# Softmax sums folded into the value products of three narrow attentions

## The chip, the cores and the metric

The kernel runs on one core of a Trainium2 chip, in one launch. The metric is device time in microseconds. The core has five engines that run their own queues in order: TensorE (PE), VectorE (DVE), ScalarE (ACT), GpSimd (POOL) and SyncE (SP, which issues DMAs). They meet through semaphores.

## What is computed

A stack of four layers over x of shape [4, 512, 128]; each is a cross attention to a short context of 154 rows a batch, followed by a mixture of experts. Three of the four cross attentions (layers 0, 2 and 3) are narrow: 16 heads of 8 columns. With layer norm and per-layer details (rotary tables and norms of q and k in layer 0, a mask in layer 2) cut, each of them is

```
q, k, v = split_heads(xn @ Wq), split_heads(ctx @ Wk), split_heads(ctx @ Wv)   # 16 heads of 8
attn    = softmax(einsum('bhqd,bhkd->bhqk', q, k) * scale, axis=-1)            # 512 x 154 a head
out     = einsum('bhqk,bhkd->bhqd', attn, v)                                   # 512 x 8 a head
x       = x + tanh(gate) * (out.reshape(B, T, 128) @ Wo + bo)
```

The softmax needs a row maximum ahead of the exponential and a row sum behind it. The other layer (1) has a wide attention, and layer 2 a causal one besides; the change doesn't touch them.

## The kernel before

`narrow_attention` is called three times, with names that begin with L0x ("rope"), L2x ("mask") and L3x ("plain"). It works through four batches b = 0 to 3. The 16 heads are four groups c of four heads; head j of a group sits in rows 32j to 32j+31. For one batch there are these pieces, and the order of PE's queue is written out by hand:

- **Scores for the maxima** (`scores`, L1149): twelve units a batch, eight of three row tiles and four of two, for the *next* batch f = b + 1. Every unit goes to the same two PSUM banks (0 and 1), so unit n waits for the DVE maximum (`maxima`, L1611) of unit n-1. I call the twelve units of a batch S0 to S11; S2, S5, S8 and S11 are the short ones.
- **Maxima turned** (`max_rows`, L1158 on PE, L1396 on ACT, then a DMA into row 9 of the query tile), so that the transposed scores come out with the maximum subtracted.
- **Transposed scores** (`scoresT`, L1175, and L1177 for the tail of 26 context rows) in five slots c = 0 to 4 of four heads each, slot 4 being the tails of all 16 heads; banks 2 to 5. ACT takes the exponential of each (`exps`, L1404) into `pT`.
- **Value products** (`products`, L1198): four matmuls a slot, 128 rows by 32 columns each, into bank OUT = 6. The weights `vz` hold 8 value columns at head c's place in a 32-column window and zeros elsewhere, so the four slots pile up in one bank.
- **Sums** (`sums`, L1210): the same four matmuls once more, with weights of ones (`oz`, and `ot` for the tail), into bank SUMS = 7. Each sum comes out 8 times, in the rows of its own head.
- **Normalising**: ACT copies both banks out (`values`, L1412 and L1413, to `ov` and `rsum`), DVE inverts and multiplies per tile t of 128 rows (`normalised`, L1622 and L1626), PE multiplies by Wo (`output`, L1225), DVE adds the residual (`added`, L1634) and takes the statistics (`kept_in_parts`).

In batch b the PE queue is: T0, P4 of the batch before, S0, max_rows, sums 4, rowsT, S1, T1, P0, S2, queries, sums 0, S3, T2, S4, P1, S5, sums 1, T3, S6, P2, output, S7, max_rows, sums 2, S8, T4, S9, P3, S10, sums 3, S11 (T and P being `scoresT` and `products` of a slot). The last batch has no S pieces. In layers 0 and 3 it also carries the first steps of the experts' router, whose DVE work stands behind `normalised` in DVE's queue and which `output` waits for. DVE's queue in a batch is the twelve maxima with the normalising of the batch before put between them. Each layer begins and ends at a barrier of all engines.

At the start of a layer ACT fills the query tiles with ones and `vz` with zeros (L1418), POOL makes regrouped weights (L990 or L992) and clears the key tile (L994), and DVE writes values into `vz` (L1561) and `vt` (L1562).

## Time and profile before

| | us |
|---|---|
| three runs | 1573.18, 1577.87, 1580.15 |
| median | 1577.87 |
| span of the profiled execution (its device time is not given apart from that) | 1592.2 |
| span above the median | 14.3 |
| L0x, first scores to the last residual added | 39.5 to 189.5 |
| L2x, the same | 738.7 to 874.4 |
| L3x, the same | 1317.5 to 1458.4 |
| mean granted TensorE clock | 0.900 |

### The profile page before, as it was taken

What the parts mean: (1) busy time and instruction counts of PE and PEld (TensorE: products, weight loads), DVE (VectorE), ACT (ScalarE), POOL (GpSimd) and SP (SyncE); (2) the same over time, 40 slices, a digit from 0 to 9 for tenths busy, and PEclk for the clock granted to TensorE, in tenths of its full rate; (3) what the DMA queues carried; (4) which work ended last, traced back from release to release, by engine and by line L of the source; (5) the groups of instructions that cost most, each with busy time, mean ns of one, the idle gap of its engine ahead of it and who ended that gap; (6) DMA issues with size and microseconds to landing.
All of it is one profiled execution on the core that took longest, in us unless ns stands there. A gap on an engine that the chain in (4) does not pass through costs nothing. (4 is left out here: it accounts for less than half of the span.)

```text
span 1592.2 us, 25277 instructions
## 1 busy us (share of the span) xinstructions
PE 1297.0 (81%) x8946; PEld 752.5 (47%) x8946; DVE 946.5 (59%) x2139; ACT 723.1 (45%) x1940; POOL 527.5 (33%) x625
## 2 busy tenths in 40 slices
PE   2799629579989977784997698989887977996998
PEld 2444317345656645463442455656554434442443
DVE  6466621444555655255664688888764875555664
ACT  3354413166656533342543465655755333454222
POOL 2320340525333361333100365656643320000444
PEclk8599859799999997895998799999988996998999
DMA  2444120330000002322000000000000001000000
GB/s 65 127 130 128 40 66 26 72 75 14 1 1 2 1 27 62 89 58 50 9 10 2 1 1 1 1 2 1 1 1 1 1 10 23 10 3 1 7 7 14
DMA packets 66991, 45.30 MB, mean 28 GB/s; under 512 B 17564, under 2 KB 60261, under 8 KB 66869
## 3 DMA queue, kind: packets, MB, share of 16 engines
q1 hardware_dynamic: 61013, 34.48, 8.4%
q0 software_dynamic: 4096, 8.40, 1.9%
q8 instruction: 74, 1.21, 0.3%
q10 hardware_dynamic: 1760, 0.82, 0.3%
q14 instruction: 48, 0.39, 0.1%
HBM read 24.91 MB, written 13.89 MB: 24 GB/s over the span
## 5 line engine op out<-in xcount | busy, mean ns | idle before, releaser
L3411 ACT ACTIVATE L2a_pr<-psum,L2a_negmax 128x512 f32<-128x512 f32 (+3 forms) x256 | 132.6, 532 | 94.0 <-DVE L2a_negmax L3537 40.1
L557 ACT ACTIVATE L1x_praw<-psum,L1x_negmax 128x154 f32<-128x154 f32 x256 | 96.5, 392 | 78.4 <-DVE L1x_negmax L649 78.2
L318 POOL TENSOR_TENSOR L1x_pm<-L1x_praw,L1x_total 128x1024 f32<-128x1024 f32 x32 | 60.7, 1898 | 160.6 <-DVE L1x_total L655 111.7
L3276 PE MATMUL psum<-ident,L2a_pr 128*128 128x128 f32 x640 | 85.9, 278 | 19.0 <-DVE L2a_pT L3550 11.7
L649 DVE TENSOR_REDUCE L1x_negmax<-psum 128x4 f32<-128x616 f32 x64 | 50.7, 794 | 55.2 <-PE psum L370 51.0
L3276 PEld LDWEIGHTS psum<-ident,L2a_pr 128*128 128x128 f32 x640 | 71.7, 143 | 24.7 <-issue 21.1
L1978 POOL TENSOR_TENSOR L3f_scaled<-L3f_sg,L3f_wide 128x512 f32<-128x512 f32 (+1 forms) x44 | 55.7, 1271 | 66.9 <-ACT L3f_sg L2057 37.9
L1611 DVE TENSOR_REDUCE L3x_negmax<-psum 128x6 f32<-128x924 f32 (+1 forms) x48 | 47.7, 1011 | 46.8 <-PE psum L1149 37.4
L1611 DVE TENSOR_REDUCE L0x_negmax<-psum 128x6 f32<-128x924 f32 (+1 forms) x48 | 47.8, 1010 | 44.9 <-PE psum L1149 40.6
L3161 POOL TENSOR_TENSOR L2a_pr<-L2a_pr,L2a_total 128x1024 f32<-128x1024 f32 x29 | 56.5, 1947 | 46.5 <-DVE L2a_total L3566 46.3
L3164 POOL TENSOR_TENSOR L2a_pr<-L2a_pr,L2a_total 128x768 f32<-128x768 f32 x32 | 48.7, 1520 | 70.0 <-DVE L2a_total L3566 69.7
L1611 DVE TENSOR_REDUCE L2x_negmax<-psum 128x6 f32<-128x924 f32 (+1 forms) x48 | 47.8, 1011 | 32.6 <-PE psum L1149 27.8
L1404 ACT ACTIVATE L3x_pT<-psum 128x512 f32<-128x512 f32 x80 | 41.4, 606 | 50.3 <-PE psum L1175 41.8
L1404 ACT ACTIVATE L2x_pT<-psum 128x512 f32<-128x512 f32 x80 | 41.4, 605 | 49.0 <-PE psum L1175 40.5
L2057 ACT ACTIVATE L3f_sg<-psum 128x512 f32<-128x512 f32 (+1 forms) x44 | 26.3, 598 | 66.8 <-PE psum L2000 66.8
L3556 DVE COPY L2a_pT<-psum 128x768 f32<-128x768 f32 (+1 forms) x64 | 54.2, 846 | 3.3 <-PE psum L3276 3.3
L370 PE MATMUL psum<-L1x_kT,L1x_qT 64*128 64x154 f32 x512 | 52.6, 327 | 3.9 <-ACT L1x_qT L538 3.0
L1404 ACT ACTIVATE L0x_pT<-psum 128x512 f32<-128x512 f32 x80 | 41.4, 605 | 30.2 <-PE psum L1175 23.6
L3411 ACT ACTIVATION_READ_ACCUMULATOR L2a_pr<-psum,L2a_negmax 128x1 f32 x256 | 53.5, 209 | 0.0
L557 ACT ACTIVATION_READ_ACCUMULATOR L1x_praw<-psum,L1x_negmax 128x1 f32 x256 | 52.9, 207 | 0.0
L2878 PE MATMUL psum<-L1f_gu,L1f_xsT 128*128 x92 | 51.2, 645 | 1.1 <-ACT L1f_xsT L2931 1.1
L2000 PE MATMUL psum<-L3f_xnT,expert_arena 128*128 128x512 f32 (+1 forms) x88 | 46.7, 614 | 4.2 <-PEq L3822 4.2
(741 smaller groups left out, 3372.1 us busy)
## 6 DMA issues: line engine op xcount, KB each, us to landing
expert_arena<-in_L_ffn_w SPq DMA_DIRECT2D x16, 256.0 KB, 4.4
group_in<-zero SPq DMA_DIRECT2D x2, 1472.0 KB, 9.3
L1f_xs<-group_in SPq DMA_DIRECT2D x10, 256.0 KB, 3.8
group_out<-L1f_ys SPq DMA_DIRECT2D x10, 256.0 KB, 3.6
L1f_gu<-in_L_ffn_gate_up_w SPq DMA_DIRECT2D x8, 256.0 KB, 3.5
slots_in<-zero SPq DMA_DIRECT2D x1, 1280.0 KB, 9.0
L0f_xs<-slots_in SPq DMA_DIRECT2D x5, 256.0 KB, 3.6
resid<-in_x SPq DMA_DIRECT2D x4, 256.0 KB, 5.8
```

The source lines that it names most:

```text
L318: nc.gpsimd.tensor_tensor(pm[:, n % 2].rearrange("p j t k -> p (j t) k"), praw[:, n % 3, :, :, 0:MAIN].rearrange("p j t k -> p (j t) k"), ...
L370: last = nc.tensor.matmul(psum[:, 2 * u + j, x * CTX:(x + 1) * CTX], qT[rows, g, t * P:(t + 1) * P], kT[rows, g, :], start=True, stop=True)
L557: nc.scalar.activation(praw[:, n % 3, j, t, :], psum[:, 2 * u + j, x * CTX:(x + 1) * CTX], ACT.Exp, bias=negmax[:, n % 2, u, j, x:x + 1], ...
L649: nc.vector.tensor_reduce(negmax[:, n % 2, u].rearrange("p j x -> p (j x)").rearrange("p (j x) -> p j x", x=2), psum[:, 2 * u:2 * u + 2, 0 ...
L1404: nc.scalar.activation(pT[:, (n % 2) * NG + j, :], psum[:, LANES + j, :], ACT.Exp, scale=scale).then_inc(s["pt"], 1)
L1611: nc.vector.tensor_reduce(negmax[:, f % 2, half, 2 * h:2 * h + 2, off:off + count], psum[:, bank:bank + 2, 0:count * CTX].rearrange("p j ( ...
L1978: nc.gpsimd.tensor_tensor(scaled[0:rows, n % 2, :], sg[0:rows, n % 3, :], wide[0:rows, picked_to(n) % SLANT, :], ALU.mult).then_inc(s["sca ...
L2878: nc.tensor.matmul(psum[:, UP[i % len(UP)], :], xsT[:, q % 2, t * P:(t + 1) * P], w["gu"][:, bass.ds(expert[i], 1), :].rearrange("p a f -> ...
L3161: ins = nc.gpsimd.tensor_tensor(x, x, inv[:, 0:2].unsqueeze(2).to_broadcast([P, 2, SEQ]), ALU.mult)
L3276: last = nc.tensor.transpose(psum[:, TURN + n // 4, n % 4 * P:(n % 4 + 1) * P], pr[:, m % RING, n * P:(n + 1) * P], core.ident[:])
L3411: ins = nc.scalar.activation(pr[:, i % RING, SEQ * j + lo:SEQ * j + hi], psum[:, bank + j, lo:hi], ACT.Exp, bias=negmax[:, i % RING, e:e + ...
L3556: nc.vector.tensor_copy(pT[:, q % 2, t:t + 7:3, heads, :], src[:, :, 0:3 * P].rearrange("p j (k x) -> p k j x", x=P))
```

## The change

The sums get no matmuls of their own. A 32-column window of `vz` has 24 columns that hold zeros; head group c now has ones in the eight columns of its neighbour c ^ 1, so that one matmul gives values and sum. Two groups would then write into each other's rows, so groups 0 and 2 go to bank EVEN = 6 and groups 1 and 3 to bank ODD = 7. In each bank half of the rows hold values and the other half sums, for the head group next door. The tail is split in the same way: `vt` is used in two halves of 64 rows, one for each bank, 8 matmuls in place of 4.

Behind it: ACT reads EVEN twice with a row mask as its scale (`half`), once for the sums and once for the values; DVE adds the ODD bank to each with the opposite mask (`odd_merged`, two scalar_tensor_tensor of 128x512); one stream shuffle of 128x512 brings each sum to its head's rows; the reciprocals stay four of 128 columns inside a batch and are two of 256 in `all_normalised`; the multiplications become two of 256 columns. In DVE's queue these are spread over the maxima anew. In PE's queue `output` moves from before S7 to behind it. POOL fills `vt` with its pattern of ones first thing in each layer, and ACT fills `vz` in four pieces from a bfloat16 pattern `windows`.

```diff
-    LANES, OUT, SUMS = 2, 6, 7
+    TAIL_AT = (0, 2, 1, 3)
+    LANES, EVEN, ODD = 2, 6, 7
...
             def _(pool):
+                nc.gpsimd.tensor_copy(vt[:].rearrange("p f j x a d -> p (f j) x (a d)"),
+                                      core.pairs[:].unsqueeze(1).unsqueeze(3).to_broadcast([P, B * NG, 2, 2 * DK])).then_inc(s["vt_ones"], 1)
                 pool.wait_ge(loaded, 16 * n_loads)
...
                         if b:
-                            pe.wait_ge(s["ov"], 2 * b - 1)
+                            pe.wait_ge(s["even"], 2 * b)
...
+                    if c == 1:
+                        if b:
+                            pe.wait_ge(s["odd"], 2 * b)
+                        elif rope:
+                            pe.wait_ge(s["kc"], 2)
                     for j in range(NG):
-                        x = c * P + 32 * j
-                        nc.tensor.matmul(psum[32 * j:32 * j + 32, OUT, :], vz[:, b, x:x + 32] if c < NG else vt[:, b, j].rearrange("p c d -> p (c d)"),
-                                         pT[:, (n % 2) * NG + j, :], start=(c == 0), stop=(c == NG))
-
-                def sums(b, c):
...
-                    for j in range(NG):
-                        last = nc.tensor.matmul(psum[32 * j:32 * j + 32, SUMS, :], core.oz[:, c, :] if c < NG else core.ot[:].rearrange("p c d -> p (c d)"),
-                                                pT[:, (n % 2) * NG + j, :], start=(c == 0), stop=(c == NG))
+                        own = slice(32 * j, 32 * j + 32)
+                        p = pT[:, (n % 2) * NG + j, :]
+                        if c < NG:
+                            x = (NG * b + c) * P + 32 * j
+                            last = nc.tensor.matmul(psum[own, EVEN + c % 2, :], vz[:, x:x + 32], p, start=(c < 2), stop=False, skip_group_check=True)
+                        else:
+                            for a in range(2):
+                                rows = slice(64 * a, 64 * a + 64)
+                                last = nc.tensor.matmul(psum[own, EVEN + a, :], vt[rows, b, j].rearrange("p x a d -> p (x a d)"), p[rows, :],
+                                                        start=False, stop=True, skip_group_check=True)
                     last.then_inc(s["pv"], 1)
...
                     for t in range(QT):
-                        pe.wait_ge(s["on"], QT * b + t + 1)
+                        if t % 2 == 0:
+                            pe.wait_ge(s["on"], 2 * b + t // 2 + 1)
...
                     products(b, 2)
+                    scores(f, 7, 8)
                     if b and not ends:
                         output(b - 1, lane(b, 3, 1))
-                    scores(f, 7, 8)
                     if f < B:
                         max_rows(2 * f, lane(b, 3, 0))
-                    sums(b, 2)
...
-                    nc.scalar.activation(ov[:], psum[:, OUT, :], ACT.Copy).then_inc(s["ov"], 1)
-                    nc.scalar.activation(rsum[:], psum[:, SUMS, :], ACT.Copy).then_inc(s["ov"], 1)
+                    nc.scalar.activation(rsum[:], psum[:, EVEN, :], ACT.Copy, scale=core.half[:, 1:2]).then_inc(s["even"], 1)
+                    nc.scalar.activation(ov[:], psum[:, EVEN, :], ACT.Copy, scale=core.half[:, 0:1]).then_inc(s["even"], 1)
...
-                def normalised(b, t0, t1):
+                def odd_merged(b, k):
...
+                    nc.vector.scalar_tensor_tensor(out=to[:], in0=psum[:, ODD, :], scalar=core.half[:, k:k + 1], in1=to[:],
+                                                   op0=ALU.mult, op1=ALU.add).then_inc(s["odd"], 1)
...
+                    v.step(nc.vector.stream_shuffle(oT[:], rsum[:], [i ^ DK for i in range(32)]))
...
-                    normalised(b - 1, 0, 1)
+                    odd_merged(b - 1, 0)
                     maxima(f, 2, 3)
-                    normalised(b - 1, 1, 2)
+                    sums_swapped(b - 1)
                     query_squares(g)
                     maxima(f, 3, 4)
+                    odd_merged(b - 1, 1)
+                    inverted_sums(b - 1, 0, 1)
                     maxima(f, 4, 5)
                     query_inverted(g)
-                    normalised(b - 1, 2, 3)
+                    inverted_sums(b - 1, 1, 2)
                     maxima(f, 5, 6)
-                    normalised(b - 1, 3, 4)
+                    normalised(b - 1, 0)
+                    inverted_sums(b - 1, 2, 3)
                     maxima(f, 6, 7)
+                    inverted_sums(b - 1, 3, 4)
+                    maxima(f, 7, 8)
+                    normalised(b - 1, 1)
                     added(b - 1)
```

## Rows read from the trace of the kernel before

**Rows 1.** The page's first part: busy time, share of the span, instructions of each engine.

```profile
PE 1297.0 (81%) x8946; PEld 752.5 (47%) x8946; DVE 946.5 (59%) x2139; ACT 723.1 (45%) x1940; POOL 527.5 (33%) x625
```

**Rows 2.** Batches 1, 2 of L3x: length; PE, PEld, DVE, ACT, POOL busy; clock; DMA.

```profile
1369.65:1400.14 30.49, 29.38 (x299) 14.11 (x295) 18.99 (x31) 13.79 (x27) 0.00 (x0) 1.00 0.07 12
1400.14:1426.27 26.13, 25.09 (x269) 12.34 (x265) 18.36 (x31) 12.83 (x24) 0.00 (x0) 1.00 0.01 3
```

**Rows 3.** PE in order of time, L3x: start, length, line, operation, idle before.

```profile
1347.27 1.61 PE L1210 MATMUL psum<-L3x_pT,oz 128*32 128x512 f32 x8
...
1369.65 1.05 PE L1149 MATMUL psum<-L3x_k,L3x_q 32*128 32x154 f32 x12
1370.63 0.60 PE L1158 MATMUL psum<-ident,L3x_negmax 128*8 128x128 f32 x4
1371.17 1.06 PE L1210 MATMUL psum<-L3x_pT,ot 128*32 128x512 f32 x8
...
1372.75 1.05 PE L1149 MATMUL psum<-L3x_k,L3x_q 32*128 32x154 f32 x12
...
1380.71 1.05 PE L1149 MATMUL psum<-L3x_k,L3x_q 32*128 32x154 f32 x12 [0.36 <-DVE L3x_negmax L1611]
...
1382.99 0.79 PE L1149 MATMUL psum<-L3x_k,L3x_q 32*128 32x154 f32 x8 [0.23 <-DVE L3x_negmax L1611]
...
1387.54 1.16 PE L1225 MATMUL psum<-L3x_wo,L3x_oT 128*128 128x128 f32 x8
1388.63 1.05 PE L1149 MATMUL psum<-L3x_k,L3x_q 32*128 32x154 f32 x12
...
1391.14 0.79 PE L1149 MATMUL psum<-L3x_k,L3x_q 32*128 32x154 f32 x8
1391.87 1.14 PE L1177 MATMUL psum<-L3x_q,L3x_k 32*32 32x512 f32 x32
1392.94 1.05 PE L1149 MATMUL psum<-L3x_k,L3x_q 32*128 32x154 f32 x12
```

**Rows 4.** DVE in order of time, L3x batch 1, same columns.

```profile
1381.81 1.12 DVE L1611 TENSOR_REDUCE L3x_negmax<-psum 128x6 f32<-128x924 f32 x1 [1.16 <-PE psum L1149]
1382.85 0.94 DVE L1622 RECIPROCAL L3x_rsum<-L3x_rsum 128x128 f32<-128x128 f32 x1
1383.83 0.29 DVE L1626 TENSOR_TENSOR L3x_oT<-L3x_ov,L3x_rsum 128x128 f32<-128x128 f32 x1
...
1388.74 0.75 DVE L1634 SCALAR_TENSOR_TENSOR L3x_oT<-psum,gate,resid 128x512 f32<-128x512 f32 x1 [0.89 <-PE psum L1225]
```

**Rows 5.** Groups of one line, L2133 (experts of layer 3): count, busy us, mean ns.

```profile
L2133 DVE STREAM_SHUFFLE L3f_wide<-L3f_shares 128x512 f32<-128x512 f32 x36 | 26.1, 727 | 0.0
```

**Rows 6.** DVE in order of time, L0x batch 0: first squares of the queries.

```profile
74.29 0.69 DVE L1569 TENSOR_TENSOR L0x_ra<-L0x_qf 128x512 f32<-128x512 f32 x1 [0.90 <-ACT L0x_qf L1361]
```

**Rows 7.** L3x batch 3 in order of time: DVE, then PE.

```profile
1433.34 3.35 DVE L1622 RECIPROCAL L3x_rsum<-L3x_rsum 128x512 f32<-128x512 f32 x1 [4.20 <-ACT L3x_rsum L1413]
...
1437.87 1.13 PE L1225 MATMUL psum<-L3x_wo,L3x_oT 128*128 128x128 f32 x8 [2.25 <-DVE L3f_lg L1875]
1449.51 1.04 PE L1210 MATMUL psum<-L3x_pT,ot 128*32 128x512 f32 x8
1455.56 2.05 PE L1225 MATMUL psum<-L3x_wo,L3x_oT 128*128 128x128 f32 x8 [5.01 <-DVE L3x_oT L1626]
```

**Rows 8.** Busy time by stretch, last batch of L2x.

```profile
850.10:853.50 3.40, 1.34 (x12) 1.25 (x16) 2.66 (x6) 0.26 (x1) 0.00 (x0) 1.00 0.00 0
853.50:856.90 3.40, 3.40 (x20) 0.60 (x20) 2.33 (x11) 1.75 (x4) 0.00 (x0) 0.50 0.02 5
```

**Rows 9.** Start of L2x in order of time: POOL, PE; below, POOL at 758.

```profile
711.82 0.39 POOL L992 COPY L2x_wqp<-L2x_wq 128x128 f32<-128x128 f32 x1 [16.58 <-POOLq L3820]
712.36 1.11 PE L1052 MATMUL psum<-L2x_wk,ctxp 128*80 128x128 f32 x4 [4.70 <-POOL L2x_wqp L992]
758.84 1.27 POOL L1040 TENSOR_TENSOR resid<-resid,L2x_gbo 128x512 f32<-128x512 f32 x1 [0.68 <-DVE L2x_xn L1537]
```

More of the change, by code:

```diff
@@ L177, in _ @@
                 last.then_inc(parts_made, 1)
+                dve.wait_ge(consts, 7)
+                nc.vector.tensor_reduce(core.half[:], core.hmask[:].rearrange("p (x a) -> p a x", a=2), X_AXIS, ALU.add)
                 dve.wait_ge(ctx_made, 2)
@@ L1176, in scoresT @@
                             else:
-                                last = nc.tensor.matmul(psum[32 * x:32 * x + 32, LANES + j, :], k4[rows, x, b, MAIN:KP], q4[rows, b % QB, x, :],
+                                to = 32 * TAIL_AT[x]
+                                last = nc.tensor.matmul(psum[to:to + 32, LANES + j, :], k4[rows, x, b, MAIN:KP], q4[rows, b % QB, x, :],
                                                         start=True, stop=True)
@@ L1269, in _ @@
                     pe.wait_ge(s["bvb"], 1)
-                    nc.tensor.matmul(psum[:, OUT, 0:D], bvb[:], w["wo"][:], start=True, stop=True).then_inc(s["bias_ps"], 1)
+                    nc.tensor.matmul(psum[:, EVEN, 0:D], bvb[:], w["wo"][:], start=True, stop=True).then_inc(s["bias_ps"], 1)
                 for b in range(B):
@@ L1308, in _ @@
                     scores(f, 5, 6)
-                    sums(b, 1)
                     scoresT(b, 3)
@@ L1328, in _ @@
                     scores(f, 10, 11)
-                    sums(b, 3)
                     scores(f, 11, 12)
@@ L1334, in _ @@
                 products(B - 1, NG)
-                sums(B - 1, NG)
                 if dispatch:
@@ L1417, in _ @@
                 filled(0)
-                nc.scalar.activation(vz[:].rearrange("p f e -> p (f e)"), core.oneb[:, 0:1].to_broadcast([P, B * NG * WIDE]), ACT.Copy,
-                                     scale=0.0).then_inc(s["vz_zero"], 1)
+                for f in range(B):
+                    nc.scalar.activation(vz[:, f * NG * P:(f + 1) * NG * P].rearrange("p (c j e) -> p c j e", c=NG, j=NG),
+                                         core.windows[:].unsqueeze(2).to_broadcast([P, NG, NG, 32]), ACT.Copy).then_inc(s["vz_ones"], 1)
                 if rope:
@@ L1735, in _ @@
                         router.spread(dve, v)
-                    maxima(f, 9, 10)
                     normed(b + 3)
@@ L1745, in _ @@
                     router.front_first(dve, v, xns[0])
-                normalised(b - 1, 0, QT)
+                all_normalised(b - 1)
                 if router:
@@ L1758, in _ @@
                     router.best(dve, v, 0, 1, 1)
-                normalised(B - 1, 0, QT)
+                all_normalised(B - 1)
                 if dispatch:
```

92 lines of the change are left out of this document (53 added, 39 removed).

## The prediction

> **What bounds the kernel now.** I read the page first: PE is busy for 81% of the span, more than any other engine [rows 1]. That is an average, and the change sits in three stages only, so the next view is the busy time by stretch of two batches of layer 3's attention [rows 2]. There PE is busy 29.38 of 30.49 us and 25.09 of 26.13 us, DVE 19 and 18. By that share every matmul taken out would come off the time. The third view, PE in order of time, says otherwise [rows 3]. Between one score unit and the next stands a piece of filler, and where the filler is a single piece PE idles 0.36 or 0.23 us until DVE's maximum frees the banks. S4 starts at 1380.71 and S5 at 1382.99: 2.28 us a long unit, and that is 0.99 of PE, 1.12 of DVE's maximum [rows 4] and some 0.17 of handing over. This ping-pong over two banks is a second bound right under PE. Eight long units at 2.28 and four short ones at about 1.75 (0.72 + 0.80 and the handing over; S8 to S9 takes 1.80 [rows 3]) make 25.2 us a batch, against the 30.49 and 26.13 measured. So of a batch's sums only what stands in a gap that is longer than its 2.28 or 1.75 can come off.
>
> **What goes.** A group of sums takes 1.0 us of PE at the high clock (1371.17 to the next piece at 1372.16, by its 1.06 less the overlap) and about 1.55 at the low one [rows 3]. There are 5 x 4 x 3 = 60: 59 us of PE's time.
>
> *Gap by gap, L3x batch 1* (S0 at 1369.65, the next at 1400.14, 30.49 [rows 2, 3]). S0 to S1 is 3.10 with max_rows, sums and rowsT; without sums it is 2.11 of PE's work, so the ping-pong's 2.28: -0.8. S1 (1372.75) to S4 (1380.71) is 7.96 [rows 3]: T1 and P0 fill the first gap to 2.9, `queries` and sums the second to 2.8, the third is the ping-pong's 2.28. The second falls to 1.8, its own 0.72 and 1.06 of `queries`: -1.0. S5 (1382.99) to S7 (1388.63) is 5.64 [rows 3], 2.7 with sums and T3 and 2.95 with P2 and `output`; the first falls to 1.75: -0.9. Sums 3 stand alone behind S10 in a gap of 2.28: 0. Sums 2 stand behind S7 and are dealt with below.
>
> **What DVE gets.** A batch had four reciprocals of 0.94 and four multiplications of 0.29: 4.9 us [rows 4]. Now there are two merges from PSUM, by the one like instruction 0.75 each [rows 4]; a shuffle, 0.73 by 36 of the same shape [rows 5]; the reciprocals; and two multiplications of 256 columns, between 0.29 and 0.69 (a 512-column one [rows 6]), say 0.42. Sum 6.8: +1.9 us. Beside a unit's 0.99 of PE and 0.17 there is room for 1.15 of DVE work in each long gap and 0.9 in each short one. Put where the diff puts them: the first merge and the shuffle fit. Behind maximum 3 stand a merge and a reciprocal, 1.7: the maximum of S4 starts 0.6 late, so the gap S4 to S5 grows from 2.28 to 2.9: +0.6. Behind maximum 5, 0.42 + 0.94 makes 0.3 more in the gap S6 to S7. The other reciprocals fit within 0.1.
>
> **The output's new place.** `output` leaves the gap S6 to S7, which falls from 2.95 to 2.28 + 0.3: -0.35. It now stands behind S7, and its second half needs the second multiplication, which DVE's queue has behind maximum 7. After S7's start that maximum ends at 2.3 and the multiplication at 2.75; only then come half of `output` (0.55), max_rows (0.53) and S8: 3.9 us for a gap that was 1388.63 to 1391.14, 2.51 [rows 3]. +1.4. PE waits there for DVE for 1.3 us in a place where it waited for nothing; behind the wait are max_rows, whose DMA has some 8 us in hand, and S8.
>
> Batch 1 in sum: -0.8 - 1.0 - 0.9 + 0.6 + 0.1 - 0.35 + 1.4 = about -1.0. The waits on `even` cost nothing: both ACT reads end about 1 us before P0 comes up, as they stood on ACT ahead of slot 1's exponentials already; `odd` is up 0.2 us before P1. In layer 0 the removal behind `queries` gives nothing, as maximum 3 waits there for the squares of the queries, which wait for ACT's copy [rows 6]; I take -0.5. Batch 2 has no `queries` and no rowsT: -0.2 - 0.8 - 0.35 + 0.6 + 1.4 = +0.6. Batch 0 has nothing to normalise: -2.7 in L3x (its first sums run at the low clock, 1.6 [rows 3]), -1.8 in L2x, where DVE has late rows to finish in the same place, -1.2 in L0x. Over three layers: batch 0 -5.7, batch 1 -2.5, batch 2 +1.8: **-6.4**.
>
> **The last batch.** No maxima here; the chain is DVE, then `output`, then T2 and the exponentials. `output` of batch 2 waited for a 512-column reciprocal (3.35), four multiplications (0.9) and the router's first step [rows 7]. `all_normalised` is merge 0.75, shuffle 0.73, merge 0.75, then twice a 256-column reciprocal (half of 3.35, 1.7) and 0.42: 6.5 in place of 4.25, and it starts about 0.7 earlier (ACT's sums are read first, and sums 4 are gone): T2 comes +1.5 late. From T2 on, PE's three pieces a slot become two, and the pace goes over to ACT's 2.07 for four exponentials: from T2 to the end of the last products 9.7 us in place of 11.6 to the end of the last sums (1438.9, the end of `output`, to 1450.5 [rows 7]). The tail behind that, from 1450.5 to `output`'s end at 1457.6 [rows 7], grows by 2.25 of DVE, less 0.5 for the order of ACT's reads: 1.6 with the two tiles of `output` that are still to come. 1.5 - 1.9 + 1.6: Sum +1.2 a layer: **+3.5**.
>
> **The clock.** In the last batch of L2x PE is busy for 1.34 us of 3.4 while it waits for `output`, and the next 3.4 us are granted 0.50; L3x idles there 2.25 us and keeps 1.00 [rows 7, 8]. With PE's wait now about 5 us long, cut by half an `output`, I expect the low clock in L3x and L0x too and a longer one in L2x. In the low stretch PE is busy throughout [rows 8], so 3.4 us at half speed lose up to 1.7: bounds 0 and 1.7 a layer, twice that for a second stretch. I take 1.5 each: **+4.4**.
>
> **The layer's start.** POOL's new copy of 512 columns stands first in its queue. In L2x PE's first matmul waits 4.70 us for POOL's L992 right behind it [rows 9]; in L3x and L0x ACT, DVE and SP wait for the pieces that follow on POOL in much the same way. A copy of 128 columns takes 0.39, a two-input one of 512 takes 1.27 [rows 9]: between 0.4 and 1.3, I take 1.15, since this is a strided one of 512. **+3.4**. ACT's four short fills in place of a long one I cost at nothing: the same columns, and the first is ready sooner.
>
> **The tail products.** Eight matmuls of 64 rows by 32 columns in place of four of 128 by 32. The nearest row is the tail of the transposed scores, sixteen of 32 by 32 with the same moving columns: 1391.87 to 1392.94, 1.07 us, as much as four full ones [rows 3]. So 0, with +1.0 each (12 in all) as the upper bound if the two row halves don't run side by side. The Trainium skill, TensorEngine Tiling (Array Packing), Key Properties, says that a change of tiling mode drains TensorE. The row doesn't show it: S8, T4 and S9 follow each other by 0.73 and 1.07 us across two such changes. By the page every removed group of sums would save two drains and the new 64-row mode would add none over the mode it replaces, so that it would speak for the change, by an amount that no row prices.
>
> **Sum.** -6.4 + 3.5 + 4.4 + 3.4 = +4.9 us, taken on the profiled execution, whose span of 1592.2 stands 14.3 above the median of the runs; all terms are stretches between barriers, so I put them on the median: 1577.9 + 4.9 = about 1583.
>
> **Rivals.** *PE is the bound after all* (faster). It would need the 1.9 us of DVE work to slip in without delaying a maximum and the wait before `output`'s second half to be short. For it: PE's 96% [rows 2]. Then batch 0 gives -5.7, batch 1 about -3 and batch 2 about -1.7 a layer, the last batch -2: 5.7 + 9 + 5 + 6 = 26 us, 1552; half of that, if one of the two holds, 1565. Against it: PE's idle times that end on DVE [rows 3]. It decides if S7 to S8 stays under 2.5 us. Chance 0.16. *The low clock spreads* (slower). Inside batches 1 and 2 PE's share falls from 96% to some 83%, with a wait of 1.3 us behind S7; if the grant falls there too, each of six batches pays a stretch like that in [rows 8], 1.7 us and the slower pieces after it, 2.5: +15, 1598. For it: the grant did fall on a share of 0.39. Against it: 83% is far above that. It decides from one lost stretch in every second batch. Chance 0.14. *The 64-row tail products run one after the other* (slower): +1.0 in 12 gaps, as behind S11 there is more filler than ping-pong: 1595. Chance 0.06. *The forecast*: the sums' 59 us were nearly all cover, and what comes off is given back on DVE. Chance 0.64.
>
> **How the numbers follow.** Within 0.5% (7.9 us, about what a measurement of this kernel can tell from none) is 1570 to 1586. Of the forecast's 0.64, whose own range is 1574 to 1592 by the bounds of copy, clock and multiplications, I put 0.46 inside, 0.17 above, 0.01 below. The first rival is faster, the other two slower. Faster 0.17, same 0.47, slower 0.36. The range 1567 to 1598 leaves out most of the first rival and the far end of the second.
>
> **What the profile after would show.** No L1210 group; S0 to S1 at 2.28; S2 to S3 at 1.8 in L2x and L3x; S4 to S5 at 2.9; S7 to S8 at 3.9 with PE waiting for the multiplication; DVE busy some 2 us more a batch; `output` of batch 2 in the last batch 1.5 us later, and the granted clock at 0.50 behind it in all three layers; PE's first matmul in L2x and L3x 1.15 us later; tail products 1.0 us. The prediction is wrong if PE hardly idles in batches 1 and 2, if the low clock lasts longer, or if waits for which the trace names no releaser move with the changed queues, which I can't price.

## The result and the profile after

The kernel after takes 1587.74 us, the median of 10 runs (1579.39 to 1598.27), beside 1577.25 for the kernel before (10 runs, 1571.47 to 1580.15): ratio 1.0076, interval 1.0053 to 1.01. It is slower by 0.8%. That lies in the range 1567 to 1598 and on the forecast's side of the old time, but about twice as far from it as the 4.9 us of the sum: outside the 0.5% that were given the largest of the three chances (0.47), and in the class that was given 0.36. Medians here and below are over all runs; ratios and intervals compare each kernel with the kernel before run beside it (medians 1575.57 to 1577.25), and leave out the few runs that are over 1.5% above the fastest of their kernel.

The first part of the page for the profiled execution after, which answers to [rows 1]:

```profile
span 1583.9 us, 24590 instructions
...
PE 1270.8 (80%) x8562; PEld 756.4 (48%) x8562; DVE 969.6 (61%) x2183; ACT 723.8 (46%) x1949; POOL 532.8 (34%) x627
```

PE has 384 matmul records fewer and is only 26 us less busy; DVE is 23 us busier. The mean granted clock fell from 0.900 to 0.882. The two spans as wholes can't be set against each other, because the span before is 14 us above its own median. The excess lies outside the change: from the last residual of L0x to the first maximum of L2x that execution takes 551.2 us, and the twelve other traces of this study take 527.1 to 532.3. So I compare stretches.

Busy time by stretch. First the kernel after, two rows for each of L0x, L2x and L3x: batch 1, from its first maximum to the next batch's, and the last batch, from the last maximum to the end of the statistics of the last rows. Columns: stretch and length; PE, PEld, DVE, ACT, POOL busy with counts; clock; DMA share and GB/s.

```profile
98.75:133.05 34.30, 29.59 (x276) 16.69 (x275) 23.07 (x38) 17.20 (x31) 5.05 (x5) 0.85 0.41 114
158.68:199.53 40.85, 27.41 (x226) 13.49 (x220) 28.37 (x87) 18.69 (x32) 9.92 (x10) 0.76 0.09 25
772.43:802.77 30.34, 26.56 (x264) 14.07 (x263) 20.41 (x33) 13.80 (x26) 0.00 (x0) 0.94 0.07 13
828.47:864.31 35.84, 21.09 (x146) 6.79 (x142) 18.38 (x39) 13.32 (x25) 0.00 (x0) 0.74 0.00 1
...
1359.53:1389.87 30.34, 26.56 (x264) 14.07 (x263) 20.40 (x34) 13.81 (x26) 0.00 (x0) 0.94 0.07 12
1415.50:1452.09 36.59, 21.83 (x158) 8.55 (x153) 22.39 (x58) 14.83 (x27) 0.00 (x0) 0.73 0.01 1
```

The same stretches of the kernel before, without L3x's batch 1, which is the first row of [rows 2] (counted there from score unit to score unit, with the same length):

```profile
97.83:130.62 32.79, 30.62 (x308) 15.42 (x307) 22.43 (x35) 17.31 (x31) 5.06 (x5) 1.00 0.46 118
156.42:191.48 35.06, 26.52 (x258) 12.01 (x252) 24.32 (x81) 18.56 (x32) 9.28 (x10) 0.90 0.09 27
787.46:817.95 30.49, 29.38 (x296) 14.11 (x295) 18.99 (x32) 13.79 (x26) 0.00 (x0) 1.00 0.07 12
843.81:876.22 32.41, 22.18 (x178) 6.91 (x172) 14.31 (x33) 12.94 (x25) 0.00 (x0) 0.86 0.00 1
1427.11:1460.26 33.15, 22.19 (x190) 8.28 (x184) 18.33 (x52) 14.62 (x27) 0.00 (x0) 0.91 0.00 1
```

Two things are to be seen. In batch 1 of L3x, PE lost 2.8 us of work (29.38 to 26.56) and the batch lost 0.15 us: the rest is idle time, and the clock of the stretch went from 1.00 to 0.94. And the three last batches together grew from 100.62 to 113.28 us, 12.7 us, with a clock of 0.73 to 0.76 in place of 0.86 to 0.91. More than the whole loss sits there. A second trace of the same queue order (the section on the start of the layer) has each of the three within 0.5 us of these.

PE in order of time in the second half of L3x's batch 1, after (answers to [rows 3]; the times in brackets are idle time ahead, and who ended it):

```profile
1374.12 1.05 PE L1154 MATMUL psum<-L3x_k,L3x_q 32*128 32x154 f32 x12 [0.30 <-DVE L3x_negmax L1618]
...
1376.73 0.71 PE L1232 MATMUL psum<-L3x_wo,L3x_oT 128*128 128x128 f32 x4 [0.91 <-DVE L3x_oT L1652]
...
1377.81 0.79 PE L1154 MATMUL psum<-L3x_k,L3x_q 32*128 32x154 f32 x8
...
1382.13 1.05 PE L1154 MATMUL psum<-L3x_k,L3x_q 32*128 32x154 f32 x12 [0.23 <-DVE L3x_negmax L1618]
1384.47 0.45 PE L1154 MATMUL psum<-L3x_k,L3x_q 32*128 32x154 f32 x2 [1.29 <-DVE L3x_negmax L1618]
...
1385.48 1.92 PE L1180 MATMUL psum<-L3x_q,L3x_k 32*128 32x512 f32 x6
1387.33 1.43 PE L1216 MATMUL psum<-L3x_pT,L3x_vt 64*32 64x512 f32 x16
1388.70 1.05 PE L1154 MATMUL psum<-L3x_k,L3x_q 32*128 32x154 f32 x12
```

S7 to S8 is 3.69 us, 0.91 of it the wait for the second multiplication, as forecast (3.9 and 1.3). The new thing is at the end: behind S10, where sums 3 stood, PE idles 1.29 us, and the transposed scores after it take 1.92 us for six records that took 1.02 at the high clock. S11 (1384.47) to the next S0 (1388.70) is 4.23 us, 2.6 before. The windows of that place and of three places in the last batch:

```profile
1384.70:1388.10 3.40, 3.40 (x24) 1.35 (x30) 0.80 (x1) 1.46 (x4) 0.00 (x0) 0.50 0.00 0
1415.40:1418.80 3.40, 3.40 (x26) 0.33 (x18) 2.00 (x6) 2.49 (x4) 0.00 (x0) 0.50 0.00 0
1425.70:1432.50 6.80, 4.67 (x20) 2.50 (x24) 5.76 (x20) 0.52 (x2) 0.00 (x0) 0.50 0.01 2
1442.70:1452.10 9.40, 2.42 (x8) 1.86 (x8) 7.90 (x17) 0.00 (x0) 0.00 (x0) 0.50 0.00 1
```

The last batch of L3x in order of time, PE, after (answers to [rows 7]):

```profile
1422.33 1.06 PE L1212 MATMUL psum<-L3x_pT,L3x_vz 128*32 128x512 f32 x8
1427.83 2.05 PE L1232 MATMUL psum<-L3x_wo,L3x_oT 128*128 128x128 f32 x8 [4.44 <-DVE L3f_lg L1914]
1429.81 2.09 PE L1180 MATMUL psum<-L3x_q,L3x_k 32*128 32x512 f32 x8
...
1446.18 1.20 PE L1232 MATMUL psum<-L3x_wo,L3x_oT 128*128 128x128 f32 x4 [5.23 <-DVE L3x_oT L1652]
```

PE stands 4.44 us ahead of `output` where it stood 2.25 us, then runs `output` and the scores of slot 2 at half speed. The releaser is the router's copy on DVE, but that copy waits only for its place in DVE's queue behind `all_normalised`, whose instructions run back to back from 1421.20:

```profile
1421.20 0.75 DVE L1628 SCALAR_TENSOR_TENSOR L3x_rsum<-psum,half,L3x_rsum 128x512 f32<-128x512 f32 x1 [3.66 <-ACT L3x_rsum L1413]
...
1427.17 0.43 DVE L1652 TENSOR_TENSOR L3x_oT<-L3x_ov,L3x_rsum 128x256 f32<-128x256 f32 x1
1427.51 0.22 DVE L1914 COPY L3f_lg<-psum 128x68 f32<-128x68 f32 x1
```

### The profile page after: what moved, and what is told of

Read it like the earlier page. It is cut to its first block and busy times, and to the rows that moved or that the text cites. A ratio compares the mean times of both kernels' runs of the same rounds, so it can differ in the third digit from the quotient of the medians.

```text
span 1583.9 us, 24590 instructions
## 1 busy us (share of the span) xinstructions
PE 1270.8 (80%) x8562; PEld 756.4 (48%) x8562; DVE 969.6 (61%) x2183; ACT 723.8 (46%) x1949; POOL 532.8 (34%) x627
## 5 line engine op out<-in xcount | busy, mean ns | idle before, releaser
L1154 PE MATMUL psum<-L0x_k,L0x_q 32*128 32x154 f32 x384 | 39.3, 337 | 17.3 <-DVE L0x_negmax L1618 11.6
L1154 PEld LDWEIGHTS psum<-L0x_k,L0x_q 32*128 32x128 f32 x384 | 30.2, 207 | 43.9 <-DVE L0x_negmax L1618 31.6
```

What stands on the lines that cost most here:

```text
L1154: last = nc.tensor.matmul(psum[:, bank + j % 2, k * CTX:(k + 1) * CTX], q4[rows, f % QB, c, t * P:(t + 1) * P], k4[rows, c, f, 0:CTX], sta ...
```

## The experiments

I began with two theories. **A**: the low clock gives the gain back; PE, relieved of the sums, idles in places where it was busy, and what follows runs at 0.50. **B**: the DVE work that was added, and `output`, which now waits for it, cost the time. Each run lists its span and mean granted clock, so I also use the time that a run spent at the low clock: 2 x span x (1 - clock), as 1.00 and 0.50 are the two levels. For the profiled execution after that is 2 x 1583.9 x 0.118 = 374 us.

### The sums' places filled again

The kernel after, with four matmuls of zero weights (adding zero to a value bank) at each of the places where sums 0 to 3 stood:

```diff
+    def cover(b, c):
+        for j in range(NG):
+            nc.tensor.matmul(psum[32 * j:32 * j + 32, EVEN + c % 2, :], core.zero[:, 0:32],
+                             core.ctxp[:].rearrange("p b k -> p (b k)")[:, 0:SEQ], start=False, stop=False, skip_group_check=True)
```

> The changed kernel with four groups of matmuls with weights of zeros, added into the same banks, at the places where sums 0 to 3 stood (48 groups of 60; the result is the same). The profiles show the granted clock low for 208 us inside the three narrow attentions after the change and for 140 before. Theory A, the clock: the loss comes from stretches at 1.2 GHz that follow PE's new idle time. Then the covers bring the low time back to some 140 to 160 us and the time down from 1587.7 to 1577 to 1583, although PE has 48 us more to do. Theory B, DVE and the waits: the loss is DVE's added work and output's wait. Then the covers give nothing or cost up to 10 us: 1587 to 1598.

1593.71 us (6 runs, 1588.15 to 1596.82), ratio 1.0103, interval 1.0084 to 1.0122. The low clock did leave: 325 us of it in the median run in place of 374, none in batch 1 of L3x. But that batch is longer:

```profile
1366.92:1398.27 31.35, 28.49 (x296) 14.03 (x295) 20.41 (x34) 13.80 (x26) 0.00 (x0) 1.00 0.07 12
```

31.35 us at the full clock, against 30.34 after and 30.49 before. With about the PE work of before and the DVE work of after the batch loses 0.9 us to the kernel before, with no low clock in it: that is theory B's part. One gap outweighs what the others gain: S7 to S8 takes 4.68 us (2.51 before), as `output`, its wait and the filler now all stand there. So A alone is out, and a filler that costs PE as much as the sums did is no cure.

### The sums dropped, nothing added

The kernel before with sums of slot 0 only, by weights of ones (the products of the later slots signal ACT in their place); the sums of slots 1 to 4 are left out, and the probabilities are divided by wrong sums. (The weights have to be ones in all columns: with `oz` as it was, three quarters of the sums would be zero and not all inverses finite.)

```diff
-                    if n < 0:
+                    if n < 0 or c:
                         return
...
-                nc.gpsimd.memset(core.oz[:], 0.0).then_inc(groups, 1)
+                nc.gpsimd.memset(core.oz[:], 1.0).then_inc(groups, 1)
```

> The kernel before, with its softmax sums made for slot 0 alone, by weights that are all ones (slots 1 to 4 are left out, so the probabilities are divided by wrong sums); nothing is added on VectorE, ScalarE or GpSimd, and the output is issued where it was. It is the change's gain without its cost on the other engines. From the gaps between maxima of batch 1 in the kernel before and after, sums cost 0.3 to 1.0 us at each of their places, 3.4 us a batch, and there is no second wait of the output: with the clock as before, some 9 us a layer, 1549 us. Theory A (the clock takes back what the freed TensorE gives): low clock appears in batches 0 and 1 and in the last batches here too, as VectorE's work is not needed for it; low-clock time in the three attentions goes from 140 us to over 190, and the time is 1556 to 1566. Theory B (the time after is set by VectorE's added work and the later output): low-clock time stays under 160 us and the time is 1545 to 1553.

1570.49 us (8 runs, 1559.76 to 1582.12), ratio 0.9976, interval 0.9947 to 1.0004. That is outside what either theory expected: 48 of the 60 groups of sums, 48 us of PE's work by the prediction's 1.0, taken out for nothing and with the queues in their old order, are worth 5 us in the median, and not even that is certain. The windows of the profiled execution, L3x: batch 1, then the last batch in two parts.

```profile
1342.25:1370.99 28.74, 25.37 (x264) 13.31 (x263) 19.00 (x32) 13.62 (x26) 0.00 (x0) 1.00 0.07 13
1395.70:1415.78 20.08, 15.43 (x134) 5.79 (x128) 11.58 (x36) 13.37 (x25) 0.00 (x0) 1.00 0.01 2
1415.78:1426.61 10.83, 3.11 (x16) 1.94 (x16) 6.76 (x16) 1.09 (x3) 0.00 (x0) 0.69 0.00 0
```

Batch 1 falls by 1.75 us only, for 4.0 us of PE's work: two bounds close to each other, as the prediction had it (PE 25.37 of 28.74 busy, the rest idle behind maxima). This execution, at 1560.32, is among its kernel's fastest: 15 us under the kernel before, with about its low-clock time (320 us by the trace). Over the eight runs low-clock time has a median of 336 us against 312 for the kernel before (61 runs), so part of A shows here without any DVE work, and by the two numbers the low clock takes back a good part of what the removal gives.

### The DVE work alone

The kernel before, with two merges and a shuffle a batch added to DVE in L2x and L3x (reading and writing spare tiles), PE untouched:

```diff
+                    src = core.ctxp[:].rearrange("p b k -> p (b k)")[:, 0:SEQ]
+                    v.step(nc.vector.scalar_tensor_tensor(out=core.x1[:, 8:12, :].rearrange("p n d -> p (n d)"), in0=src, scalar=core.gate[:, 0:1], in1=src, op0=ALU.mult, op1=ALU.add))
...
+                    v.step(nc.vector.stream_shuffle(core.x1[:, 8:12, :].rearrange("p n d -> p (n d)"), core.ctxp[:].rearrange("p b k -> p (b k)")[:, 0:SEQ], [i ^ DK for i in range(32)]))
```

> The kernel before with DVE's added work alone in layers 2 and 3: two scalar_tensor_tensor and a shuffle of 128x512 into a tile that nobody reads, near the places where the change has them; PE's queue untouched. 2.2 us more of DVE in each of eight batches. Theory A: PE stays busy, so batches 1 and 2 grow by 0.6 each and the last by 2 x 2.2 a layer: 2 x (1.2 + 4.4) = 11 us at most, half of it if PE's own pace hides it: 1583 to 1588, with the low clock within 10 us of before. Theory B: the same 11 us or more, and it is the whole of the loss: 1588 to 1592. It tells how large DVE's share is.

1581.16 us (7 runs), ratio 1.0034, interval 1.0017 to 1.005: some 5.5 us for two layers. Low-clock time stays at 310 us in the median run. In L3x batch 1 goes from 30.49 to 30.55 and batch 2, which has less PE filler, from 25.80 to 26.98 (from its first to its last maximum):

```profile
1380.60:1407.58 26.98, 24.82 (x266) 12.17 (x266) 20.33 (x36) 12.01 (x22) 0.00 (x0) 1.00 0.01 2
```

So B's cost is real, of that order, and has nothing to do with the clock.

### The start of the layer

The kernel after, with POOL's pattern copy moved from the head of its queue to behind the clearing of `k4`:

```diff
-                nc.gpsimd.tensor_copy(vt[:].rearrange("p f j x a d -> p (f j) x (a d)"),
-                                      core.pairs[:].unsqueeze(1).unsqueeze(3).to_broadcast([P, B * NG, 2, 2 * DK])).then_inc(s["vt_ones"], 1)
                 pool.wait_ge(loaded, 16 * n_loads)
...
                 nc.gpsimd.memset(k4[:], 0.0).then_inc(s["k_zero"], 1)
+                nc.gpsimd.tensor_copy(vt[:].rearrange("p f j x a d -> p (f j) x (a d)"),
+                                      core.pairs[:].unsqueeze(1).unsqueeze(3).to_broadcast([P, B * NG, 2, 2 * DK])).then_inc(s["vt_ones"], 1)
```

> The kernel after, with GpSimd's copy that fills the tail tiles with their pattern moved behind the clearing of k4, so that it no longer stands ahead of the layer's first work on that queue. The prediction gave it 3.4 us for three layers. If that is right: 1584 against the 1587.5 of the kernel after. If it is hidden, as the two prologues in the traces say (L3x 33.35 before and 32.60 after): 1586 to 1589, and each prologue within 0.5 us of the kernel after where the clock is the same.

1586.7 us (4 runs, 1582.21 to 1590.92), ratio 1.0075, interval 1.0052 to 1.0098: not to be told from the kernel after. In the trace after, PE's first matmul of L2x waits 5.30 us behind POOL, where it waited 4.70 [rows 9]:

```profile
702.75 1.11 PE L1057 MATMUL psum<-L2x_wk,ctxp 128*80 128x128 f32 x4 [5.30 <-POOL L2x_wqp L997]
```

With the copy moved it is 4.72 again. So the copy costs this wait 0.6 us, its own length (0.61 us on GpSimd), half of the 1.15 forecast. With four runs a term of 1 to 2 us in all can't be excluded; 3.4 looks too much.

### The idle places filled

The kernel after, with five of the zero-weight groups (5 x 4 matmuls) ahead of the `output` that PE waits for in the last batch:

```diff
                     if ends:
+                        for _ in range(5):
+                            cover(b, 0)
                         output(b - 1, 1)
```

> The changed kernel with five groups of zero-weight matmuls in the last batch of each narrow attention, between P0 and output, where PE otherwise waits for DVE. Theory A: of the low time in the last batches (19.7, 18.8 and 19.5 us in the three layers after, 7 to 9 before) some 7 to 10 us a layer go, and the time falls by 5 to 10 us: 1578 to 1583. Theory B: the fills stand in a wait for DVE and change nothing: 1586 to 1590.

1590.78 us (5 runs, 1583.95 to 1592.37), ratio 1.0085, interval 1.0062 to 1.0107: no gain. Yet the last batches in its profile did what they should:

```profile
161.44:198.82 37.38, 26.38 (x266) 12.02 (x260) 28.15 (x87) 18.69 (x32) 9.46 (x10) 0.87 0.09 26
838.01:871.44 33.43, 22.57 (x186) 7.84 (x180) 18.38 (x39) 13.32 (x25) 0.00 (x0) 0.81 0.01 1
1423.41:1457.49 34.08, 22.39 (x198) 8.90 (x192) 22.39 (x58) 14.77 (x27) 0.00 (x0) 0.87 0.00 1
```

104.89 us in place of 113.28. The 8.4 us came back elsewhere: low-clock time was 372 us in the median run, as before the edit (374). The profiled execution is the median one, and beside the trace of the kernel after it shows where: 2 to 4 us more in each batch 1 of L0x and L2x and in batch 2 of L3x, all with more low clock (12.0 us of it in L2x's batch 1 where there were 3.4), and 4 us more between L0x and L2x. Then both: the last batch filled, and one group between S10 and S11 of every batch.

```diff
                     scores(f, 10, 11)
+                    cover(b, 3)
                     scores(f, 11, 12)
```

> The kernel after, with matmuls of zero weights (four of 512 columns for one group, adding zero) at two places: one group between scores 10 and 11 of every batch, where TensorE idles 1.29 us and behind which the low clock began in batch 1, and five groups ahead of the last batch's output. Theory A (the low clock gives back what the change gains): the gap S11 to S0 in batch 1 goes from 4.13 (4.51 in L0x) to 2.93, no low clock in batch 1, the three last batches as in the kernel with the last groups alone (35.6, 32.7, 32.3 us from the last maxima on), so some 8 us there and 4 us in the batches: 1575 to 1580. Theory B (VectorE's work and the output's wait): the filling work only costs, 1588 to 1594. Rival to both: the low clock moves to a place that is not filled (batch 0, the prologue), its sum in the attentions stays near 208 us and the time is 1584 to 1590.

1589.65 us (6 runs, 1575.24 to 1597.03), ratio 1.0104, interval 1.0074 to 1.0133. The profiled execution is the fastest of the six and shows the place as A had it: the filler costs nothing (S10 to S11 is 2.35 us, 2.34 without it), and the transposed scores behind it run at full speed.

```profile
1376.10 1.05 PE L1154 MATMUL psum<-L3x_k,L3x_q 32*128 32x154 f32 x12 [0.23 <-DVE L3x_negmax L1626]
1377.09 1.06 PE L1222 MATMUL psum<-ctxp,zero 128*32 128x512 f32 x8
1378.45 0.40 PE L1154 MATMUL psum<-L3x_k,L3x_q 32*128 32x154 f32 x2 [0.30 <-DVE L3x_negmax L1626]
...
1380.03 1.09 PE L1216 MATMUL psum<-L3x_pT,L3x_vt 64*32 64x512 f32 x16
1381.05 1.05 PE L1154 MATMUL psum<-L3x_k,L3x_q 32*128 32x154 f32 x12
```

```profile
1353.51:1382.22 28.71, 25.93 (x272) 13.64 (x271) 20.39 (x34) 13.80 (x26) 0.00 (x0) 1.00 0.07 13
```

The batch is 28.71 us in place of 30.34 with one low stretch less: 1.6 us is what one stretch cost. But the median of the kernel did not move; its other runs had mean clocks down to 0.878. The rival that was written down, that the low clock turns up where nothing is filled, is what the medians say. Where it went in those slower runs of this kernel no trace shows, since only the profiled one has a trace.

### The second multiplication earlier

```diff
+                    normalised(b - 1, 1)
                     maxima(f, 7, 8)
-                    normalised(b - 1, 1)
                     added(b - 1)
```

> The kernel after, with the second multiplication of the normalised rows (L1652) issued on VectorE before maxima 7 in place of behind them, so that the output in batches 1 and 2 need not wait its 0.91 us for it (gap S7 to S8 3.42 us). Theory B (this wait and the order on VectorE set the time): the gap falls to about 2.6, 0.8 us in each of 6 batches is gained, 1583. Theory A (the clock takes it back): the gap falls, but low-clock time moves to another place, 1585 to 1589. A third outcome: maxima 7 come later by the 0.42 us of the multiplication, scores behind them wait, and the gap before is longer by what this one is shorter.

1573.19 us (10 runs, 1565.1 to 1592.07), ratio 0.9992, interval 0.9963 to 1.0021. I ran it again:

> The kernel with the second multiplication ahead of maxima 7 once more, beside the two that move the output, since its runs spread from 1565 to 1592. If its median of 1573.2 holds, 1570 to 1577 here, and the spread goes with the mean granted clock of each run: some 0.4 us of span for each us of low clock.

1573.76 us (12 runs, 1565.71 to 1590.51), ratio 0.9975, interval 0.9954 to 0.9996. One swap of two instructions on DVE gives back all that the change lost, 14 us, more than either theory expected. The first of its two traces says how. `output` is one piece again, right behind S7, and batch 1 runs at the full clock:

```profile
1363.79 1.05 PE L1154 MATMUL psum<-L3x_k,L3x_q 32*128 32x154 f32 x12 [0.30 <-DVE L3x_negmax L1618]
1364.78 1.16 PE L1232 MATMUL psum<-L3x_wo,L3x_oT 128*128 128x128 f32 x8
...
1366.30 0.79 PE L1154 MATMUL psum<-L3x_k,L3x_q 32*128 32x154 f32 x8
```

```profile
98.64:130.17 31.53, 27.73 (x276) 16.48 (x275) 22.98 (x38) 17.20 (x31) 5.04 (x5) 0.89 0.42 117
768.84:796.38 27.54, 24.68 (x264) 13.42 (x263) 20.31 (x33) 13.80 (x26) 0.00 (x0) 1.00 0.08 13
1349.19:1376.73 27.54, 24.67 (x264) 13.41 (x263) 20.32 (x33) 13.80 (x26) 0.00 (x0) 1.00 0.08 13
```

S7 to S8 falls from 3.69 to 2.51, so 1.2 us, and the batch from 30.34 to 27.54, 2.8: the other 1.6 is the low stretch at its end, which is gone though nothing was put behind S10. A wait in one place cost clock in another, 8 us later. All traces together bear that out. Take the place behind S10 in batches 1 and 2 of L2x and L3x, four a trace. In the four traces that have both the wait ahead of S8 and the one behind S10 (after, pattern copy moved, last batch filled, output later alone) 13 of 16 such places get a low stretch. In the three that have only the one behind S10 (this edit twice, both edits) none of 12 does, in the two where S10 is followed by filler none of 8, and in the three with the sums' matmuls in place (before, DVE work added, before with the output later) none of 12. With the sums dropped, where PE idles behind S10 too, two of four do. So the wait of 1.3 us is followed by the low clock mostly where 0.9 us were idle ahead of it; what spared the three others isn't shown.

The two traces of this one kernel, 1571.06 and 1584.03, also say where the slower one loses its time. L0x, from its first maximum to its last residual, takes 146.0 us in the first and 165.2 us in the second, with 50 and 90 us of low clock. That is more than the whole difference.

### The output of batch 2 later

In the last batch, `output` was moved from ahead of the scores of slot 2 to behind those of slot 3, in the kernel after, in the kernel after with the multiplication's edit, and in the kernel before:

```diff
-                    if ends:
-                        output(b - 1, 1)
                     scores(f, 3, 4)
...
                     scoresT(b, 3)
+                    if ends:
+                        output(b - 1, 1)
```

> The kernel after, with the output of batch 2, which is issued inside the last batch, moved on TensorE's queue from ahead of scores of slot 2 to behind those of slot 3. In the kernel after TensorE stands 4.44 us (L3x, 1423.39 to 1427.83) ahead of this output, and the scores of slot 2, which need nothing of it, stand behind it. Theory A with its refinement (in the last batches TensorE's queue is held by the output, which is late by VectorE's longer chain; the idle time also brings the low clock): the slots 2 and 3 come 3 to 4 us earlier, exps of the last batch end 2 to 3 us earlier in each of three layers, low-clock time in the last batches falls from 58 us to under 45, and the time is 1575 to 1580. Rival (the order behind it is held by ScalarE's exps anyway, and the later output delays VectorE's work behind it): 1585 to 1590.

1577.09 us (12 runs, 1565.53 to 1592.3), ratio 0.9987, interval 0.9965 to 1.0008. That is some 10 us under the kernel after, as expected. The last batches:

```profile
161.07:201.24 40.17, 25.10 (x226) 11.27 (x220) 28.02 (x87) 18.79 (x32) 10.07 (x10) 0.76 0.09 24
834.25:863.40 29.15, 18.32 (x146) 6.32 (x142) 18.37 (x39) 13.31 (x25) 0.00 (x0) 0.79 0.00 1
1414.49:1444.56 30.07, 19.66 (x158) 7.64 (x153) 22.40 (x58) 14.82 (x27) 0.00 (x0) 0.78 0.01 2
```

6.7 and 6.5 us less in L2x and L3x, 0.7 in L0x. There the move makes a new wait. DVE adds the residual only behind `output`, and the router's mask stands behind that in DVE's queue, so PE now waits for the mask, in this trace for 5.38 us:

```profile
182.90 0.17 PE L2376 MATMUL psum<-L0f_mask,L0f_tri 128*128 128x8 bf16 x1 [5.38 <-DVE L0f_mask L2360]
```

> Both edits: the kernel after with the second multiplication ahead of maxima 7, and the output of batch 2 behind the scores of slot 3 in the last batch. If the two are independent and the idle time of TensorE is what both take away: 1573.2 (the multiplication's edit alone) less some 8 us: 1563 to 1568, under the kernel before. If the clock takes back what is gained: 1570 to 1576.

1564.16 us (6 runs, 1557.49 to 1572.54), ratio 0.9918, interval 0.9889 to 0.9948: the version that beats both. The gains of the two edits nearly add up: 14 and 11 us alone, 23.6 together, from 1587.74. PE in the last batch of L3x has no wait ahead of `output` any more:

```profile
1418.01 2.04 PE L1180 MATMUL psum<-L3x_q,L3x_k 32*128 32x512 f32 x8
1420.10 1.13 PE L1232 MATMUL psum<-L3x_wo,L3x_oT 128*128 128x128 f32 x8
```

> The kernel before with the same move of the output in the last batch, and nothing else. Its idle time ahead of that output is 2.25 us in L3x. If the stall is a cost of its own that the change only made longer: some 1.5 us a layer, 1570 to 1573, so about half of what the same move gives to the kernel after. If it is within the noise: 1574 to 1577.

1573.85 us (12 runs), ratio 0.9992, interval 0.9977 to 1.0006: not to be told from none, at most 3.6 us. The trace shows that this is a sum of two things and not nothing: the last batches of L2x and L3x are 3.8 and 2.3 us shorter than in the kernel before, and that of L0x is 5.8 us longer, with 4.51 us of waiting for the router's mask and 5.5 us more low clock. The kernel after gained 10 us by the same move, since its DVE chain ahead of `output` is longer. The move in L2x and L3x alone, which these numbers suggest for both kernels, was not run.

### The clock over all runs

Medians over the runs of each kernel; low is time at the low clock worked out per run, slope is the span's by it within the runs of that kernel:

```
kernel                        runs   time us   clock            low us   slope
before                          61   1576      0.898 to 0.909   312      0.25
before, output later            12   1573.85   0.896 to 0.907   311      0.22
before, DVE work added           7   1581.16   0.899 to 0.905   310      0.31
before, sums dropped             8   1570.49   0.888 to 0.897   336      0.57
after                           10   1587.74   0.877 to 0.889   374      0.37
after, pattern copy moved        4   1586.70   0.880 to 0.886   368      0.37
after, sums' places filled       6   1593.71   0.895 to 0.903   325      0.32
after, last batch filled         5   1590.78   0.879 to 0.888   372      0.26
after, S10 and last filled       6   1589.65   0.878 to 0.895   368      0.37
after, output later             12   1577.09   0.872 to 0.894   365      0.34
after, multiplication early     10   1573.19   0.879 to 0.897   358      0.40
the same again                  12   1573.76   0.879 to 0.894   351      0.43
after, both edits                6   1564.16   0.880 to 0.893   348      0.35
```

The kernel after has 62 us more low clock than the kernel before. By its own slope that is 23 us, against the 10 to 12 measured: at equal clock the change would have gained some 11 us. This is an estimate, and a loose one: no run of the kernel after had as little as 312 us, and by the slope of the kernel before the 62 us are 16, which leaves a gain of 4. That the slopes are what the low clock costs, and not only what goes with it, is argued and not shown.

## Why the prediction was right, and where its sizes were off

**The sign and the range: right.** The sums' matmuls were mostly cover and not the bound. The dropped sums show it: 48 us of PE's work are 5 us of time in the median and 15 in the profiled execution. That the number came within 6 us owes something to luck, as the batches alone were off by 8 us. The rival *PE is the bound after all* (1552 to 1565) fell.

**The gaps: right to 0.4 us.** S0 to S1 was forecast at 2.28 and is 2.35 (1358.35 to 1360.70); S2 to S3 1.8 and 1.78; S4 to S5 2.9 and 2.49; S7 to S8 3.9 and 3.69, with PE waiting 0.91 for the multiplication where 1.3 was forecast. DVE's batch grew by 1.42 us (18.99 to 20.41), not 1.9. At the full clock batch 1 of L3x takes 28.71 us with the filled idle time: -1.8, where the prediction had -1.0. The trace with the pattern copy moved has it at 28.72 with nothing filled. Batch 2, forecast at +0.6, came out at -0.2.

**The batches' sum: wrong in size.** Forecast -6.4 over three layers. Measured between the two profiled executions, batch 0, 1, 2: L0x -0.8, +1.5, -0.2; L2x +1.3, -0.1, -0.2; L3x +0.3, -0.1, -0.2. Together +1.6. The terms that failed are batches 0 and 1, and not by their gaps but by their clock, which the prediction took to stay as it was: by the clock of the two traces L3x had 18.5 us at the low level in batch 0 where it had had 11.6, and each batch 1 has at least one stretch (0.94 in the windows above, 0.85 in L0x). Batch 0 is the less certain of the two, as it differs between traces of one order: L2x's has no low clock in the trace before and 7.1 us of it, and 2.8 us more time, in that of the kernel before with the output later. The lost stretches of batch 1 are the rival *the low clock spreads*. So are those behind S10 of batch 2 in L2x and L3x, which the windows above count with the last batch (1415.40:1418.80 in L3x). Five of its six batches have one; the price is 1.6 us for the one that could be measured alone, not 2.5. Its 14% were too few: the argument against it weighed the share of a whole batch (83%), and the grant fell behind S10, where PE now waits 1.29 us in a gap that the prediction had put at nothing, some 8 us after the wait ahead of S8 that it had priced.

**The last batches: chain right, clock half.** Forecast +3.5 for the chain and +4.4 for the clock. Measured +12.7. With PE's wait filled they are 104.89, so the chain is at most +4.3 and the clock at least +8.4 (by the clock column the filled batches still have 31 us of low clock where those before had 22), beyond 1.5 a layer and within the bound of 1.7 for each of two stretches. The wait ahead of `output` was forecast at about 5 us and is 4.44. What the prediction priced as one stretch of 3.4 us is 6.8 us there (1425.70 to 1432.50), 3.4 more ahead of it, and 9.4 at the tail, where 6.0 us were low before too.

**The start: too high.** +3.4 forecast. The copy takes 0.61 us, where 1.15 was taken, and the wait of L2x grew by 0.6. From GpSimd's first instruction of the layer to its first maximum L0x takes 29.9 us in place of 28.2, with 6 us more low clock, and L3x 16.9 in place of 17.1: there the copy is hidden. L2x takes 23.0 us, against 21.4 to 22.2 in three traces of the old order (28.9 in the trace before, which is the odd one there). In all some +2.5. **The tail products: right.** 1.09 us for eight at the full clock, nothing added; the rival of their running one after the other fell. With the terms as measured, +1.6, +12.7 and +2.5 make 16.8 by the traces; the medians say 10.5 and the ratio 12. Of the difference 2.8 us hang on the choice of the trace before (L2x's batch 0); the rest isn't accounted for.

**What stays open.** Why a given wait is followed by the low clock and another isn't, and where the low clock goes when a place is filled. Filling all places lowered the low clock and cost more in work than it gave; filling the last batch, or that and S10, left both medians where they were. The two edits that removed waits by order lowered the time by 14 and 11 us and the median low clock by 9 to 23, of which, by their slopes, 3 to 10 us is clock and the rest the waits themselves. L0x, whose batch 1 takes 31.5 to 40.8 us in the traces of the versions after, is the least steady of the three, and none of the edits was aimed at it.

## What to carry to other kernels

When PE is 96% busy and still in lockstep with another engine over a pair of banks, drop the work you mean to save and time that first: it tells what the removal is worth with the queues as they stand (here 0.2 to 0.3%) before any replacement is built. It is no ceiling: with two waits moved as well the new version is 0.8% under the old one, though the same move of `output` alone gave the old one next to nothing. Work taken from PE leaves idle time, and idle time on this chip may cost more than itself, because the work behind it may run at half speed; so move the waits as well as the work, first those where a queue is held by an instruction whose input became later. Look at every layer when a block is moved: in the old kernel L0x's router waited behind the later `output` and took back what L2x and L3x had gained. Padding the idle time with empty matmuls cured the place and not the kernel; reordering two instructions on VectorE and one block on TensorE gave 1.5%.

## What the runs showed of the hardware

Each us of low clock goes with 0.22 to 0.57 us of span, and its total varies by 20 to 76 us between runs of one kernel on one core: most of the spread of the runs goes with it (1565 to 1592 us for the early multiplication, correlation 0.93 with the low time). Removing waits of 0.9 us each, twice a layer, changed the median by 14 us. The Trainium skill, TensorE: Matmul & The Clock Gate, The HAM clock gate, says that the clock is gated by how busy TensorE has recently been; the traces agree in direction (0.50 behind the waits of 1.29 and 4.44 us, 1.00 where they were filled), though not at every place (a wait of 1.3 us behind S10 was followed by 0.50 at 13 of 16 places with a wait of 0.9 us ahead of it, and at none of 12 without), and the price of a place isn't to be read from that place alone.

A reciprocal of 128x256 takes 1.74 us, one of 128x128 0.94, so one instruction for two tiles saves 0.14 us over two; the merge from PSUM takes 0.75 and the shuffle 0.72 for 128x512, as the rows before had it. Eight matmuls of 64 rows by 32 columns take as long as four of 128 by 32 (1.09 and 1.07 us).
